# Attention on one core: Q's projection moves ahead of V's on TensorE, and their evacuations trade places on ScalarE

## What is computed

```python
k = jnp.einsum('ahe,bce->bach', W_K, x)      # x: the layer norm of the input
q = jnp.einsum('ahe,bce->bach', W_Q, x)
v = jnp.einsum('ahe,bce->bach', W_V, x)
scores = jnp.einsum('bach,baCh->bacC', k, q)
masked = jnp.tril(scores) - 10000000000.0 * (1.0 - mask)
attn = jax.nn.softmax(masked / np.sqrt(d_head), axis=-1)
z = jnp.einsum('bach,bacC->baCh', v, attn)
out = jnp.einsum('ef,bcf->bce', W_O, z_flat)
```

## Time and profile before

| | |
|---|---|
| runs | 1354.89, 1351.04, 1348.25 us; median 1351.04 |
| profiled execution | 1348.61 us, span from first to last instruction 1346.7 us |
| TensorE busy | 1208.7 us (90% of the span) |
| VectorE busy | 912.4 us (68%) |
| ScalarE busy | 829.2 us (62%) |
| GpSimd busy | 505.1 us (38%) |
| attention stage, 30 to 520 us | TensorE 481.84, ScalarE 424.79, VectorE 401.38 us busy of 490 |

### The profile page before, as it was taken

One profiled execution on the slowest core, in us unless ns is written; L12 is line 12 of the kernel. 1 busy time (PEld: TensorE's weight loads), 2 busy tenths in 40 slices (PEclk: granted clock), 3 DMA queues, 4 the chain that ended last, 5 costly groups with the idle time before them and its releaser, 6 DMA issues. The chain is left out here.

```text
span 1346.7 us, 26854 instructions
## 1 busy us (share of the span) xinstructions
PE 1208.7 (90%) x7787; PEld 917.0 (68%) x7787; DVE 912.4 (68%) x3538; ACT 829.2 (62%) x2478; POOL 505.1 (38%) x619
## 2 busy tenths in 40 slices
PE   6999999999999998799985999999996988199990
PEld 5666666666666665599973777777774656199990
DVE  6788888887878785444436888888873667234445
ACT  6898888888888886144432555656554665044440
POOL 2111324142414131545541344433432376545550
PEclk9999999999999999799996999999997999599995
DMA  9100000000000000222221000000000011222226
GB/s 291 49 2 1 12 7 11 7 13 6 16 7 13 5 13 1 72 69 71 69 64 62 17 16 17 17 1 1 1 1 0 15 39 40 76 59 73 69 71 195
DMA packets 54442, 52.89 MB, mean 39 GB/s; under 512 B 7341, under 2 KB 43098, under 8 KB 54330
## 3 DMA queue, kind: packets, MB, share of 16 engines
q1 hardware_dynamic: 36320, 29.39, 7.7%
q0 software_dynamic: 8928, 17.84, 3.9%
q10 hardware_dynamic: 9082, 4.33, 1.1%
HBM read 29.48 MB, written 22.05 MB: 38 GB/s over the span
## 5 line engine op out<-in xcount | busy, mean ns | idle before, releaser
L1354 ACT ACTIVATE prob<-prob,negmax 128x256 f32<-128x256 f32 (+3 forms) x512 | 283.2, 556 | 47.6 <-DVE negmax L1448 47.5
L1448 DVE CUSTOM_DVE_ANT_0 prob<-bank,mask 128x256 f32<-128x256 f32 (+3 forms) x512 | 223.9, 480 | 41.9 <-PE bank L1164 41.6
L1524 POOL TENSOR_TENSOR Vs<-Vh_sb,rinv 128x512 f32<-128x512 f32 x64 | 66.6, 1041 | 365.7 <-DVE rinv L1426 365.7
L1050 POOL DMA_INDIRECT expert_out<-f_x_yb,f_x_to x142 | 136.7, 963 | 153.0 <-DVE f_x_yb L1038 118.3
L1176 PE MATMUL bank<-prob,Vs 128*64 128x512 f32 (+3 forms) x1024 | 152.0, 439 | 0.5 <-POOL Vs L1524 0.4
L678 POOL DMA_INDIRECT expert_in<-f_xn,f_slot x128 | 126.9, 991 | 49.1 <-issue 31.2
L982 PE MATMUL bank<-f_x_xbT,W_sb 128*128 128x256 f32 x568 | 138.3, 387 | 1.7 <-DVE f_x_xbT L1018 1.7
L1003 ACT ACTIVATE f_x_hid<-bank,cols 128x256 f32<-128x256 f32 x144 | 63.8, 474 | 92.1 <-PE bank L982 92.1
L982 PEld LDWEIGHTS bank<-f_x_xbT,W_sb 128*128 128x128 f32 x568 | 104.6, 194 | 14.8 <-DVE f_x_xbT L1018 2.9
L1003 ACT ACTIVATE prob<-bank,cols 128x256 f32<-128x256 f32 x140 | 62.0, 473 | 79.6 <-PE bank L982 79.6
L1176 PEld LDWEIGHTS bank<-prob,Vs 128*64 128x64 f32 x1024 | 63.6, 136 | 69.7 <-issue 60.0
(11 more groups left out here) (263 smaller groups left out, 3181.2 us busy)
## 6 DMA issues: line engine op xcount, KB each, us to landing
f_x_xb<-expert_in SPq DMA_DIRECT2D x73, 130.0 KB, 2.2
b_crows<-expert_out SPq DMA_DIRECT2D x16, 256.0 KB, 2.7
c_crows<-expert_out SPq DMA_DIRECT2D x16, 256.0 KB, 4.2
expert_out<-f_x_yb,f_x_to POOLq DMA_INDIRECT x142, 2.5
expert_in<-fill ACTq DMA_DIRECT2D x16, 130.0 KB, 2.5
x_sb<-in_L_attn_a_x_dram SPq DMA_DIRECT2D x8, 256.0 KB, 6.7
W_sb<-in_L_ffn_W_dram SPq DMA_DIRECT2D x1, 2048.0 KB, 10.2
expert_in<-f_xn,f_slot POOLq DMA_INDIRECT x128, 2.3
```

The source lines that it names most:

```text
L1050: pool.indirect_dma_start(yg, bass.IndirectOffsetOnAxis(ap=self.to[:, t:t + 1], axis=0), self.yb[:, t, :], None).then_inc(self.stored[t], 16)
L1354: nc.scalar.activation(mine, mine, ACT.Exp, scale=-1.0, bias=negmax[:, g % 2, i, a:a + 1], accum_out=rowsum[:, g % 2, i, a:a + 1]).then_in ...
L1448: nc.vector.tensor_tensor_reduce(out=prob[:, g % 2, a, columns(i)], in0=score_bank(i, a), in1=mask[:, T - width[i]:], scale=-1.0, scalar=H ...
```

## The change

On TensorE `project_Q` moves from behind `between` to straight behind the scores, with a wait for one mask of its own (the first, which frees `bankQ`); `project_V` follows with its wait for two masks, then `between`. On ScalarE `evac_Q` moves one exponential ahead, behind the third, and `evac_V` one back, behind the fourth; the evacuations of the row's transposes (g = 3 and 4) move with `evac_V`.

```diff
                             if ahead_too:
                                 quarter, part = V_of(g)
+                                pe.wait_ge(masked, START + (b * PAIRS + g) * PER_PAIR + 1)
+                                project_Q(*here)
                                 pe.wait_ge(masked, START + (b * PAIRS + g) * PER_PAIR + 2)
                                 project_V(u if quarter < NT else 1 - u, quarter % NT, part)
                             between(b, u, g, first, last)
-                            if ahead_too:
-                                project_Q(*here)
                             if g >= 2:
                                 out_of(b, g - 2)
...
-                                if j == 2:
+                                if j == 2 and ahead_too:
+                                    evac_Q(*here)
+                                if j == 3:
                                     if ahead_too:
                                         quarter, part = (g + 1) // 2, (g + 1) % 2
...
                                     if g == ROUTE_TR and not first:
                                         route.norm.act_evacuate(act, b - 1, 1 - u, route.xnT_ready)
-                                if j == 3 and ahead_too:
-                                    evac_Q(*here)
                                 if j == 5 and ahead_too:
                                     evac_K(*here)
```

## The result

The changed kernel takes **1377.95 us** (median of 1373.56 to 1380.73), the kernel before 1351.72 in the same series: a ratio of **1.018**, 95% interval 1.015 to 1.022 (taken from the single runs; the two medians give 1.019). The forecast was 1379, with a range of 1368 to 1387. The profiled execution took 1373.56 us with a span of 1371.6. One execution further down, of the kernel with V in its own bank, took 2070.56 us at a mean granted clock of 0.553 and is left out of that kernel's median and ratio.

A forecast was written before the change was run, and what follows sets the result against it. The attention stage was taken to run at TensorE's pace, busy 481.84 of 490 us. Six rows 20.4, last row 2.3 and first row 5.4 sum to 28 us more: 1376.6, or 1379 beside the median; range 1368 to 1387.

The forecast's parts named there:

- The ring: Plain pair: V's evacuation at 4.30 delays K's projection, PV and the next scores, 3.84 us from its start; 0.62 us more.
- the slack before the change: Plain pair before the change: V's evacuation ended at 3.71, 0.7 us before K's first matmul, so K's wait cost nothing.
- The places of a row: Pair lengths at g = 0 to 7 of a full row, forecast one by one: together 3.40 us more per row.
- g = 4: Fifth pair of a full row, where VectorE comes late: 2.30 + 1.74 + 5.03 = 9.07 us against 8.48, 0.59 more.
- The first row: Row without route work: plain at g = 2 and 4 to 7, other amounts at 0, 1 and 3; 5.4 us more.
- g = 1: Second pair of the program's first row, where K waits already: V's later evacuation was to cost the whole 1.19 us.
- the rival of the falling clock: Idle TensorE lowers its granted clock; a tenth of the attention stage at the lower level gives about 1427 us; chance 0.03.
- The sum: Whole attention stage: 20.4 for six rows, 2.3 for the last, 5.4 for the first, 28 us more.
- The signs that were named: Profile after: K waits about 0.6 us in 40 or more pairs, plain pairs 8.1, TensorE busy near 480, clock 1.00.
- gain of 0.11: Q's first matmul, 0.50 against K's 0.39 because Q waited for zT_lo: 0.11 us goes if TensorE comes last.
- TensorE alone: Rival: V's evacuation ends before K's turn, only gains stay, 1.5 us a row with half of 0.9 at g = 4 and 7; 1340; chance 0.04.
- It comes out even: Rival: waits removed at g = 4 and 7 pay for most of a 0.2 us stall; 1351 to 1357 us; chance 0.05.

The follow-up runs named there:

- TensorE's half: Against the kernel before: only TensorE's order changed, Q's projection first, then V's, then the small job; ScalarE's order as before. 1357.27 us, ratio 1.005.
- ScalarE's half alone: Against the kernel before: only ScalarE's order changed, Q's evacuation behind the third exponential, V's behind the fourth; TensorE's order as before. 1448.73 us, ratio 1.073.

## Why the prediction was right, step by step

**The ring.** V's evacuation was put at 4.30, K's wait and what is queued behind it at 0.63, 0.90 and 2.31; measured 4.30, 0.64, 0.89 and 2.30. The table above shows that this sum holds at four places of V's evacuation, 3.80 to 5.12. By the same sum the slack before the change was 7.52 - 3.84 - 3.11 = 0.57 us rather than the 0.7 of the prediction, since it is K's load that waits and not K's first matmul. And what is evacuated second had no microsecond to spare: in TensorE's half ScalarE waits for V's matmuls and gets their data at 3.80, half a microsecond ahead of 4.30. Neither changes the forecast.

**The places of a row**, in us:

| g | before | forecast | after |
|---|---|---|---|
| 0 | 7.51 | 8.14 | 8.11 |
| 1 | 7.51 | 8.14 | 8.14 |
| 2 | 7.89 | 8.14 | 8.15 |
| 3 | 7.93 | 8.50 | 8.48 |
| 4 | 8.48 | 9.07 | 8.95 |
| 5 | 8.41 | 8.33 | 8.30 |
| 6 | 7.52 | 8.14 | 8.13 |
| 7 | 8.44 | 8.65 | 8.68 |

(g = 7 is that of the row before.) The forecast's column is 3.4 us above the first in sum, the last one 3.25. The one place that is off is g = 4. The forecast let the first exponential start at 2.30; it starts at 2.18 (187.56, pair from 185.38), because K's low part of g = 3 came at 7.55 (184.45, pair from 176.90) rather than 7.68:

```profile
184.45 0.68 DVE L1416 TENSOR_TENSOR K_lo<-bank,K_hi 128x512 fp32r<-128x512 f32 x1
187.56 0.51 ACT L1354 ACTIVATE prob<-prob,negmax 128x256 f32<-128x256 f32 x1 [1.47 <-DVE negmax L1448]
```

**The first row** was mis-sized: 67.90 us from its first scores to the next row's, before 60.18, so 7.7 where 5.4 was forecast. The term at fault is g = 1, 1.19 forecast and 3.5 measured. The second pair there, TensorE and ScalarE:

```profile
23.20 0.50 PE L454 MATMUL bank<-a_xnT_hi,WVO_hi 128*128 128x512 f32 x1 [1.59 <-ACT Vh_sb L1330]
25.66 0.58 PE L1164 MATMUL bank<-Q_hi,K_hi 64*128 64x256 f32 x2 [1.50 <-DVE K_lo L1416]
29.47 0.79 PE L454 MATMUL bank<-a_xnT_hi,A_hi 128*128 128x512 f32 x1
32.40 0.60 ACT L1330 ACTIVATE Vh_sb<-bank 128x512 f32<-128x512 f32 x1
36.32 0.38 PE L1164 MATMUL bank<-Q_hi,K_hi 64*128 64x256 f32 x2
```

The scores take 3.81 us (25.66 to 29.47) rather than 2.10, at half the clock, and V's evacuation comes 6.74 after their start rather than at the forecast's 4.45 (3.26 and 1.19). From there to the next scores it is 3.92, near the 3.84 again. So the rival of the falling clock was real, at one place and for some 2.3 us.

**The sum.** The start of the program's last pair moved from 516.40 to 544.97, 28.6 us; the first row gave 7.7 (5.4 forecast), six rows 19.0 (20.4), the last row up to its last pair 2.5 (2.5), and the first scores of the program came 0.6 us earlier. That 28.6 meets the forecast's 28 so closely is partly luck: the first row took 2.3 more than forecast, the six rows 1.4 less, and the start was 0.6 early. The span grew by only 24.9, since what follows the stage happened to take 3.7 us less in this execution; in the second pair of profiles the span grew by 29.2 (1374.1 against 1344.9). The medians differ by 26.2.

**The signs that were named.** K's load waits for V's evacuation 55 times (40 or more were forecast; in a plain pair 0.91 us at the load and 0.47 at the matmul, where about 0.6 was forecast), plain pairs take 8.1, g = 5 is no longer than before, the clock from 40 to 500 us is 1.00: as forecast. Two signs were wrong. Q's first matmul stays at 0.50, since Q's is now the load that stands in the open behind the scores; the gain went to V's first matmul, 0.28 now, before:

```profile
192.03 0.38 PE L454 MATMUL bank<-WVO_hi,a_xnT_hi 128*128 128x256 f32 x1
```

That the gain of 0.11 exists is seen in the three kernels with plain pairs of 7.39, against 7.51. And TensorE's busy time in the stage is 490, not near 480: a plain pair counts 7.66 us of busy time (202.63 to 210.76), where it counted 7.52. The last output matmul ahead of the wait is counted to its modelled end, 0.40, where the next one used to start after 0.23, K's first takes 0.50 rather than 0.39, and V's first takes 0.10 less. The busy time rose, but no work was added.

**The rivals.** *TensorE alone*, with 1.5 us a row and 1340, was priced too high as well as not being what happened. With K's wait removed the time was 1351.8, and 1344.4 only when the row's job was also put ahead of V: 1.1 us a row. The term that failed most is its half of 0.9 us at g = 4: 0.2 was to be had there (8.31), and nothing at all without moving the job; g = 7 gave 0.35 (8.09). *It comes out even* needed a stall of 0.2 and gains at g = 4 and 7: the stall was 0.61, and both places got longer (8.95, 8.68). *The clock*: the stage itself stayed at 1.00 although TensorE stands still in each plain pair, and it did so in ScalarE's half alone, at 394.39 us busy from 40 to 500 us. The Trainium skill (TensorE: Matmul & The Clock Gate, "A second HAM failure mode: psum-queue depth-cycling") ties an up-and-down clock to such short pauses between groups of matmuls; from 40 to 500 us this trace doesn't agree, at 437.75 us busy of 460.

## What to carry to other kernels

Where an evacuation empties a bank that the next projection writes, its place in the evacuating engine's queue is part of TensorE's critical ring: find the start of the evacuation at which the wait begins to cost (here an estimate of 3.55 after the scores, 7.39 less 3.84), and charge each exponential put ahead of it beyond that in full, once per pair. When such a wait is taken away, look for what it was hiding before counting the gain: here the row's transposes, which had moved back with V, were next in line, and in two kernels K's own evacuation, late in ScalarE's queue. A swap written in two engines' orders is one change; half of it cost nearly four times the whole.

## What was not expected of the hardware

The granted clock fell to 0.50 for 3.5 us in the second pair of the program in both profiles of the changed kernel, after two pauses of TensorE of 1.59 and 1.50 us with a few matmuls between them (in the first profile 0.96 us busy of 3.5), while DMA was busy throughout. In the kernel before there is one longer pause instead, and the clock stayed at 1.00. Then follows the kernel with only Q ahead of the small job, with one pause too and the clock at 0.51:

```profile
25.82 0.39 PE L1164 MATMUL bank<-Q_hi,K_hi 64*128 64x256 f32 x2 [2.29 <-DVE K_lo L1416]
25.48 0.58 PE L1164 MATMUL bank<-Q_hi,K_hi 64*128 64x256 f32 x2 [2.54 <-DVE K_lo L1415]
```

Of the seven other kernels at this place, each profiled once, only the one with V's evacuation behind Q's kept 1.00, after pauses of 0.88 and 1.81. From 25.5 to 29 us ScalarE's half and the one with V's an exponential later show 0.50, V in its own bank 0.72, TensorE's half 0.80 and the last kernel, with the row's job ahead of V, 0.85. So the number of pauses does not separate them; what does stays open. From 40 us on, every plain pair of the changed kernel has a pause of about 0.5 us, and the clock is 1.00.
